# Unread products of constants in TensorE's waits between first layer, experts and second layer

## What is computed

```python
x = layernorm(x + attn(x, x, x, causal=True))
x = layernorm(x + attn(x, ctx, ctx))
p = softmax(x @ rw + rb); topw, topi = top_k(p, 2); topw = softmax(topw)
combine = zeros(T, 8).at[arange(T)[:, None], topi].add(topw)
h = gelu(einsum('td,edf->etf', x, w1) + b1)
eo = einsum('etf,efd->etd', h, w2) + b2
x = layernorm(x + einsum('etd,te->td', eo, combine))
# second layer
q, c = rmsnorm(x, g_q), rmsnorm(ctx, g_c)
x = rmsnorm(x + attn(q, c, c, mask), g_out)
```

## Time and profile before

| what | value |
|---|---|
| median of 3 runs | 594.2 us (594.09 to 597.36) |
| profiled execution | 590.02 us |
| its span, first to last instruction | 588.2 us |
| mean granted TensorE clock | 0.937 |
| TensorE busy | 518.5 us (88%) |
| DVE, ACT, POOL busy | 431.1, 363.8, 205.7 us |

### The profile page before, as it was taken

How to read it: one execution, slowest core, us unless ns; L and a number is a source line. 1 busy time by engine, 2 the same in 40 slices (tenths; PEclk the granted TensorE clock), 3 DMA queues, 4 the chain that set the end, 5 groups by cost and what they waited for, 6 DMA issues and landing times.

```text
span 588.2 us, 17011 instructions
## 1 busy us (share of the span) xinstructions
PE 518.5 (88%) x6536; PEld 378.8 (64%) x6536; DVE 431.1 (73%) x818; ACT 363.8 (62%) x716; POOL 205.7 (35%) x357
## 2 busy tenths in 40 slices
PE   6878779999999999998699993899999999999985
PEld 4756357676767767686467772467667676767763
DVE  7799978777777779876361126878989897978753
ACT  2556357777776776777334432476767667676663
POOL 8553123122130337353133002436547373530101
PEclk9789679999999999999869996699999999999998
DMA  6337478657747365465302310357373743528000
GB/s 162 102 116 210 156 194 250 171 183 180 205 144 196 130 193 153 137 183 175 95 2 86 91 37 15 101 157 218 141 185 125 190 151 108 168 69 228 12 3 17
DMA packets 41117, 79.99 MB, mean 136 GB/s; under 512 B 9327, under 2 KB 19247, under 8 KB 41055
## 3 DMA queue, kind: packets, MB, share of 16 engines
q1 hardware_dynamic: 41054, 79.16, 46.7%
HBM read 58.95 MB, written 20.13 MB: 134 GB/s over the span
## 4 chain that ended last, share of the span: by engine, by line
PE 57%; DVE 19%; ACT 8%; issue 8%; POOL 3%; DMA 3%; SPq 1%; ACTq 1%; POOLq 0%; DVEq 0%
PE bank L442 11%; PE bank L420 10%; PE bank L408 9%; PE bank L1302 5%; PE bank L376 4%; PE bank L370 4%; PE bank L1291 4%; DVE mx L609 4%; PE bank L364 3%; DVE qfix L601 2%; ACT qfix L539 2%; DMA k_scratch<-kparts 2%; PE bank L382 2%; ACT scratch L562 2%; DVE weights L1490 1%
## 5 line engine op out<-in xcount | busy, mean ns | idle before, releaser
L609 DVE TENSOR_REDUCE mx<-bank 112x1 f32<-112x500 f32 x384 | 245.3, 673 | 45.8 <-PE bank L408 42.8
L562 ACT ACTIVATE scratch<-bank 125x448 f32<-125x448 f32 x384 | 203.6, 548 | 111.9 <-PE bank L420 110.1
L408 PE MATMUL bank<-krep,qfix 96*112 96x500 bf16 (+1 forms) x384 | 153.6, 410 | 5.3 <-DVE mx L609 2.7
L420 PEld LDWEIGHTS bank<-qfix,krep 99*128 99x128 bf16 (+1 forms) x1536 | 107.6, 101 | 73.3 <-issue 26.0
L420 PE MATMUL bank<-qfix,krep 99*128 99x112 bf16 (+1 forms) x1536 | 140.1, 215 | 15.3 <-ACT qfix L539 10.1
L442 PE MATMUL bank<-scratch,v 125*32 125x112 f32 x3072 | 94.0, 262 | 0.0
L442 PEld LDWEIGHTS bank<-scratch,v 125*32 125x32 f32 x3072 | 70.2, 109 | 9.2 <-ACT scratch L562 0.6
L735 POOL TENSOR_TENSOR oT<-comb,rec 128x56 f32<-128x56 f32 x32 | 10.0, 312 | 175.0 <-DVE rec L631 175.0
L408 PEld LDWEIGHTS bank<-krep,qfix 96*112 96x112 bf16 (+1 forms) x384 | 51.5, 136 | 29.3 <-issue 18.6
L724 POOL TENSOR_TENSOR kparts<-k_rest,kparts 128x500 bf16<-128x500 f32 x48 | 54.3, 1139 | 43.1 <-ACT kparts L546 42.8
L1302 PEld LDWEIGHTS bank<-scratch 128*112 128x112 f32 x256 | 32.7, 182 | 16.0 <-issue 10.7
(11 more groups left out here) (172 smaller groups left out, 706.3 us busy)
## 6 DMA issues: line engine op xcount, KB each, us to landing
krep<-k_scratch SPq DMA_DIRECT2D x192, 187.5 KB, 4.0
k_scratch<-kparts SPq DMA_DIRECT2D x16, 1125.0 KB, 4.5
ctx_tile<-in_ctx SPq DMA_DIRECT2D x16, 750.0 KB
scratch<-in_L_xattn_e_w SPq DMA_DIRECT2D x16, 256.0 KB, 3.1
Q<-q_scratch SPq DMA_DIRECT2D x12, 168.0 KB, 3.1
q_scratch<-scratch SPq DMA_DIRECT2D x6, 168.0 KB, 2.5
Q<-q_scratch SPq DMA_DIRECT2D x12, 56.0 KB, 2.3
k_rest<-in_selq SPq DMA_DIRECT2D x1, 576.0 KB, 11.1
```

The lines of the kernel that those rows point to most:

```text
L408: nc.tensor.matmul(row_bank(v, c, lead)[0:PQ, 0:KB], qfix[0:KR[l], slot, p * PQ:(p + 1) * PQ], krep[0:KR[l], slot, p, n * KB:(n + 1) * KB] ...
L420: ins = nc.tensor.matmul(SCORES[c % 2][:, p * PQ:(p + 1) * PQ], krep[0:KS[l], slot, p, c * KP:c * KP + 128], qfix[0:KS[l], slot, p * PQ:(p ...
L562: nc.scalar.activation(P[:, p_slot(s_, slot), :], SCORES[slot % 2][0:KP, 0:UQ], ACT.Exp, scale=SCALE).then_inc(z["exp_ok"], 1)
L609: nc.vector.tensor_reduce(mx[:, par, c // NKB, c % NKB:c % NKB + 1], row_bank(v, c, lead)[0:PQ, 0:KB], AX.X, ALU.max).then_inc(z["row_max" ...
```

## The change

A helper `pe_fill(n, ps)` issues n products of `identb` (128 x 128) with the first 512 columns of `selq` into the PSUM bank `ps`. It waits for nothing, signals nothing, and nothing reads the results. It is called four times on TensorE: 5 products ahead of the wait for `oT_ok` after the first layer's attention, 8 behind the projection of the last tile and ahead of the wait for `x_ok`, 20 after the experts ahead of the wait for the first tile, 10 between that tile's queries and the selection of the first unit's queries.

```diff
+        def pe_fill(n, ps):
+
+            for _ in range(n):
+                nc.tensor.matmul(ps[:, :], identb[:, :], selq[:, :, :, :].rearrange("p i a n -> p (i a n)")[:, 0:512],
+                                 start=True, stop=True)
...
             pe_attend(pe, 0, {2: lambda: project_self(TT - 1), 4: last_var, 8: other_tiles, 10: other_queries})
+            pe_fill(5, bank[0])
             pe.wait_ge(s["oT_ok"], TT + 2)
             project_heads(pe, 0, [TT - 1]).then_inc(s["y_ps"], 1)
 
+            pe_fill(8, bank[0])
             pe.wait_ge(s["x_ok"], X_CA)
             pe_xT(pe, x_new, bank[0], ALL)
             pe.wait_ge(s["xT_ok"], 4)
...
+            pe_fill(20, bank[0])
             pe.wait_ge(s["x_ok"], X_RMS[0])
             pe_xT(pe, x_new, first_xT, FIRST)
             pe_query(pe, 1, 0)
+            pe_fill(10, bank[1])
             pe_first_queries(pe, 1)
```

## The result

The changed kernel takes **589.93 us** (median of 7 runs, 587.29 to 591.80), the kernel before 594.09 (7 runs, 590.68 to 597.36): a ratio of 0.9934, 95% interval 0.9907 to 0.9962. That is 4.2 us, some 2 to 5.5 by the interval. Timed once more, at the end of the study, it was 590.03 against 592.98, ratio 0.9953 (0.9929 to 0.9977). The forecast was 591.4 in a range of 587.5 to 595.0. Executions in a slower state, more than 1.5% above the fastest of the same kernel, are left out of the medians and ratios of this document.

The account below looks back on a forecast made before the run. TensorE was taken to bound the attention, with half clock around two waits where other engines' work covers the fills. First place 1.9 plus second 0.9 made 2.8 us off 594.2, giving 591.4 us, range 587.5 to 595.0.

Parts of the forecast that it names:

- The fills' own cost: 43 added products on TensorE's queue: 0.215 us each at full clock, all hidden behind other engines' work, none late.
- First place: First layer's last L387 to the router's sum on DVE (A): clock holds to the router's products, gaining 1.9 us.
- the lower bound: Before the router's sum: L870, L1291 and router products take 2.47 us at full clock, gain 1.73; upper bound 2.1.
- The cap: Router's sum to experts' last second product (E): expert 1 waits for DVE's gates, so 1.7 us gained there counts nothing.
- its sign in the trace: Before expert 1's first L1302: TensorE idle 1 to 2 us, starting right behind DVE's copy L1598.
- the new fall in the gelu wait: Clock falling again from 295.4 to 297.7: up to 1.7 us on expert 0's four steps, already idle time.
- Second place: Experts' last product to layer 2's first row maximum (B): L1028 saves 0.67 us, first L408 0.21, together 0.9.
- The bound of zero: Before the second layer: gain 0 if the clock falls before 365.5, where L1028 starts.
- C counted as nothing: Layer 2's first row maximum to first value product: half-clock stretch may shift by up to 3.2 us either way; taken as 0.
- The slower rival: All four groups: fills run at 1.2 GHz, come late and cost 6.2 us, giving 600.4 us; chance 0.06.
- 9.5 us of half clock: Around both waits: 9.3 + 9.7 us of matmuls at 1.2 GHz, at most 9.5 us to gain, most off the path.

Follow-up runs that it names:

- gelu wait filled: Changed kernel plus 3 products behind the transposes and 10 behind the second hidden product; 589.99 us, 0.9944 of the kernel before.
- both, again: Second run of the changed kernel plus 13 products around the gelu wait and DVE's x_new copy moved ahead of the router's sum; 588.66 us, 0.9906 of the kernel before.
- narrow products: Changed kernel with all 43 products in place but 56 columns each instead of 512; 593.27 us, 1.0005 of the kernel before.
- last groups only: Changed kernel without the 5 and 8 products, keeping the 20 and 10; first run 594.62 us, 1.0019 of the kernel before; again 592.71, 0.9972.
- fill in POOL's wait: Changed kernel plus 4 products in each layer's wait between leading rows and first transposed scores; 590.70 us, 0.9956 of the kernel before.

## Why the prediction was right, step by step

- *The fills' own cost.* Forecast 0.215 us each and nothing on the path. Measured 379 ns of modelled duration, but from start to start (4.48 - 0.38)/19 = 0.216 us in the third group, and every wait behind a group still ends with DVE or ACT. The price of the Trainium skill, 131 ns ("TensorE: Matmul & The Clock Gate", "Back-to-back issue gap") does not hold here, by these 0.216 us: this stream, with a weight load for each product, runs at the L408 rows' pace.
- *First place, 1.9 us.* Measured 1.87 us in A (8.04 to 8.08 in each of the runs with these groups, against 9.94). By terms of the chain: L870 0.40, L1291 0.84, the router 0.62, against 0.51, 0.94 and 0.28 at the lower bound and half of each at the upper. The sum was right; that the errors of its parts cancel is luck. It also took the one profile before for all: against the other profiles without the groups the gain is up to 2.4 us (10.44), since half clock there began earlier and took in the projection (L1062, 1.20 us in that profile against 0.69).
- *The cap.* Right: the copy's end moved by the same 1.87 us as the router's sum, and E did not change. But its sign in the trace was not the one named. I had said TensorE would idle 1 to 2 us at the wait. It did not in this profile, because the clock fell at 298.6 and half clock in the first expert steps used up the slack; that is the new fall in the gelu wait which the prediction had allowed for at no cost. The run with the gelu wait filled shows the idle time (1.6 us).
- *Second place, 0.9 us.* Measured 0.80 to 0.82 in B. The term that was too large is L1028: 0.57 us less (1.33 to 0.76), not 0.67: it does not halve with the clock. The remaining 0.23 us lie between it and the first maximum, where the first L408 was put at 0.21. One run (both, again) had the clock fall right behind the selection, at 367.9, and a B of 12.11: 0.62 us of the gain stay when only what follows the selection runs at half clock. The bound of zero was for a fall ahead of the selection; that is the run with narrow products (from 365.57, B 12.74, gain nothing).
- *C counted as nothing, in both directions.* In the profiled pair it is 1.09 us less (18.45 to 17.36), in the changed kernel's second profile 0.86 (17.59). Held at full clock it is 16.34. Counting it as an uncertainty was right in size; that it is even in both directions is not shown (the two kernels without wide products have two of the three longest).
- *Sum.* Forecast 2.8 us, traces 1.87 + 0.80 = 2.67, timings 4.2 and 2.95 us. The profiles taken whole agree with the timings: from L387 to the end of the span it is 301.40 and 301.58 us in the kernels before and with narrow products, 297.38 and 298.22 in the two profiles of the changed kernel, 3.2 to 4.2 less. What lies over the sum is, as far as the profiles show, C's share (0.7 to 1.1 us), and in some executions A's 0 to 0.5 and E's 0 to 1.1 us in the kernels without the first groups. Their mean over runs is not known: a profile is one execution. The forecast of 591.4 is 1.5 us above the measured 589.93: the two places were summed rightly, and these terms were left at nothing.
- *The slower rival* (half clock during the fills) occurred in no profile: the change's four groups ran at 1.00 wherever they were in place at full width. Products that are mostly zeros did hold the clock here.

## What to carry to other kernels

Filling a wait of TensorE pays what the path behind it gets from the clock, so walk that path to the first wait on another engine: here it was 2.7 us of the 9.5 us of half clock, because other engines' work (the gates, the norms) ran beside most of it. Where two chains meet, shortening one shows nothing; do both in one run before dropping either. And compare profiles from event to event: the fourteen profiles come to L387 anywhere from 286.8 to 292.6 us, though only one of them has an edit ahead of it.

## What was not expected of the hardware

The clock's steps do not belong to the kernel's steps. The same instructions in the first place had their fall at 298.6, at 303.0 or not at all, and after a fall at 294.7 half clock lasted for 17 us. Nor was it only idle or thinly used stretches behind which the clock fell: ahead of 298.6 TensorE was busy for 2.27 of 3.10 us, where the prediction had found 1.09 to 1.59 of 3.40 ahead of its falls.

And a transfer in the first layer held TensorE up by 0.2 to 2.1 us in the fourteen profiles. From the first value product of that layer to L387 twelve of them take 200.1 to 200.2 us and this wait, so that it is nearly all that differs there. The other two, last groups only (first run) and fill in POOL's wait, take 201.6 and 201.7 us and this wait; they are the two in which the clock fell right behind it. So the 2.5 us saved ahead of it by the fill in POOL's wait were in good part returned.
